# Weighted layer of a four-layer graph network: 21 dense blocks of 125 targets instead of 22, and 61 gathered groups instead of 60

## The reference, cut to what matters

```
msgs = x[src] * edge_weight[:, None]
agg  = segment_sum(msgs, dst, num_segments=6250)
out  = concat([x, agg], axis=-1) @ mlp_w.T + mlp_b
x    = layernorm(x + out)
```

## Time and profile before

| | |
|---|---|
| median of three runs | 3292.46 us |
| profiled execution, time / span | 3296.23 us / 3294.4 us |
| PE busy over the span | 2884.0 us (88%) |
| POOL busy over the span | 2196.1 us (67%) |
| DVE, ACT busy | 1772.5 us (54%), 1134.6 us (34%) |
| weighted stage, first gather to first result product | 1509.40 to 2142.84 us |

### The profile page before, as it was taken

One profiled execution on the slowest core, in us unless ns is written; L12 is line 12 of the kernel. 1 busy time (PEld: TensorE's weight loads), 2 busy tenths in 40 slices (PEclk: granted clock), 3 DMA queues, 4 the chain that ended last, 5 costly groups with the idle time before them and its releaser, 6 DMA issues. The chain is left out here.

```text
span 3294.4 us, 63759 instructions
## 1 busy us (share of the span) xinstructions
PE 2884.0 (88%) x23799; PEld 2539.8 (77%) x23799; DVE 1772.5 (54%) x5488; ACT 1134.6 (34%) x1749; POOL 2196.1 (67%) x2185
## 2 busy tenths in 40 slices
PE   1699999999899999997999999987988788877886
PEld 0377777787688878776999999977977777777776
DVE  6899997233433343437777777545433333333333
ACT  2655555000200010105666666534422222222221
POOL 4466652777477757766777777627777777777773
PEclk9799999999999999998999999968988888888886
DMA  7355555787777876772222222123222222222222
GB/s 165 122 189 176 200 190 196 265 286 273 246 250 251 286 269 231 264 257 67 47 47 48 48 48 47 39 64 80 55 53 46 53 52 46 54 45 54 53 45 55
DMA packets 163982, 433.29 MB, mean 132 GB/s; under 512 B 63603, under 2 KB 105513, under 8 KB 143580
## 3 DMA queue, kind: packets, MB, share of 16 engines
q1 hardware_dynamic: 93998, 304.72, 25.9%
q0 software_dynamic: 69680, 124.50, 17.2%
HBM read 335.49 MB, written 93.53 MB: 130 GB/s over the span
## 5 line engine op out<-in xcount | busy, mean ns | idle before, releaser
L829 POOL DMA_INDIRECT work_all<-parts_dram,idx_all x768 | 824.0, 1073 | 349.0 <-issue 227.6
L1423 PE MATMUL ps<-arena 128*128 128x288 bf16 x7154 | 1024.7, 288 | 1.2 <-DMA arena<-blocks_dram 1.2
L2045 POOL DMA_INDIRECT arena<-table,idx_all x696 | 660.9, 950 | 283.0 <-issue 210.2
L1423 PEld LDWEIGHTS ps<-arena 128*128 128x128 bf16 x7154 | 712.1, 100 | 176.2 <-DVE arena L1026 1.5
L2387 PE MATMUL ps<-M,arena 128*128 128x96 f32 x1664 | 419.6, 352 | 176.0 <-DVE arena L2256 173.1
L1591 POOL DMA_INDIRECT arena<-table,idx_all x400 | 396.8, 992 | 121.9 <-issue 121.0
L2387 PEld LDWEIGHTS ps<-M,arena 128*128 128x128 f32 x1664 | 320.0, 239 | 195.7 <-issue 194.1
L1838 PE MATMUL ps<-work_all,gathot 128*128 128x245 f32 x1100 | 312.4, 379 | 10.1 <-issue 4.4
L1846 PE MATMUL ps<-arena,X 128*96 128x125 f32 x2156 | 317.0, 272 | 3.1 <-ACT arena L1633 3.1
L1254 PE MATMUL ps<-arena,spare 128*128 128x245 bf16 x975 | 291.8, 306 | 29.8 <-ACT arena L882 17.3
L1846 PEld LDWEIGHTS ps<-arena,X 128*96 128x96 f32 x2156 | 278.3, 164 | 26.7 <-ACT arena L1633 4.6
(11 more groups left out here) (415 smaller groups left out, 4420.1 us busy)
## 6 DMA issues: line engine op xcount, KB each, us to landing
arena<-blocks_dram SPq DMA_DIRECT2D x117, 1568.0 KB
blocks_dram<-arena SPq DMA_DIRECT2D x39, 1568.0 KB, 5.8
arena<-table,idx_all POOLq DMA_INDIRECT x1096, 2.5
parts_dram<-arena SPq DMA_DIRECT2D x28, 504.0 KB, 3.2
work_all<-parts_dram,idx_all POOLq DMA_INDIRECT x768
arena<-eaT_dram SPq DMA_DIRECT2D x10, 624.0 KB, 5.3
eaT_dram<-arena SPq DMA_DIRECT2D x48, 104.0 KB, 2.5
arena<-qtable SPq DMA_DIRECT2D x104, 45.0 KB
```

The source lines that it names most:

```text
L829: eng.indirect_dma_start(out=gat_rows[kk % 3][:, u, :], out_offset=None, in_=parts_dram[:, :], in_offset=bass.IndirectOffsetOnAxis(ap=idx_ ...
L1423: last = nc.tensor.matmul(apply_ps[n % 2], blk[m % 3][:, b, :], Hs[:, b, :], start=b == 0, stop=b == NB - 1)
L2045: eng.indirect_dma_start(out=rows[g % NROW][:, u, :], out_offset=None, in_=table[:, :], in_offset=bass.IndirectOffsetOnAxis(ap=idx_all[:, ...
```

## The change

The block count goes down by one, and the first gathered group moves from 44 to 43. `NODEW` becomes 2625, the built tiles 525 instead of 550, the gathered groups 61. Since 525 is odd, the half-width room for the fp16 column list is rounded up; the pieces of `TAB` behind it move by some words. The positions in `STEPS`, `GROUP_AT`, `EDGE_AT` and `NODE_AT` follow from the constants.

```
-    WBLK, WFIRST = 22, 44
+    WBLK, WFIRST = 21, 43
...
-        wkey, wslo, wslo_h, wwin = in_tab(NTW), in_tab(NTW), in_tab(NTW // 2).bitcast(fp16), in_tab(NTW)
+        wkey, wslo, wslo_h, wwin = in_tab(NTW), in_tab(NTW), in_tab(-(-NTW // 2)).bitcast(fp16)[:, 0:NTW], in_tab(NTW)
```

## The result

The changed kernel takes 3302.43 us (median of nine runs, 3296.95 to 3311.06) against 3292.74 us for the kernel before in the same nine rounds: ratio 1.0035, 95% interval 1.0024 to 1.0045, slower by 9.7 us at the medians. A second set of twelve runs gave 3299.24 against 3293.33 us, ratio 1.0020 (1.0007 to 1.0032), slower by 5.9. The forecast was 4.1 us slower with a range of 3288 to 3304: the sign, the bound and the stated range held, the size was too small. The forecast's own range, 3293 to 3301, holds the second median and not the first; the chances gave 0.66 to a time that cannot be told from no change and 0.23 to slower, and slower came.

The account below looks back on a forecast made before the run. POOL, with no free time, was taken to become the bound, PE's gain turning into waits. + 10.3 - 4.2 - 0.2 - 1.8 = + 4.1 us on the median 3292.46 gave 3296.6 us; range 3288 to 3304.

Parts of the forecast that it names:

- What bounds the kernel: Weighted stage: PE and POOL go at one pace, 10.30 us per group; POOL has no free time and becomes the bound.
- The waits: PE at `sums` in the weighted stage: idle for the DMA in front of most groups, some 20 us in all.
- The first rival: TensorE stays the bound of the weighted stage, so the time falls by 20.0 us to 3272.5; chance 0.07.
- PE's own need: PE's own time for the changed weighted stage, from first gather to `result_product`: 613 us.
- The clock: Rival: PE's waits lower its granted clock; under 0.96 PE is the bound again, at 0.94 the time is 3311; chance 0.11.
- One group more on POOL: Eight more indirect DMAs on POOL in the weighted stage: one more period, + 10.3 us.
- The end: Slack of 6.04 us between POOL's last issue and the last `sums` shrinks to 1.85, swallowing 4.2 us.
- the shorter tail: From the last `sums` to `result_product`: 17 applies instead of 18 behind the last group, 0.2 us less.
- POOL's own stalls: POOL's indirect DMA issues in the weighted stage: fewer key pairs on DVE shorten the 21.6 us of stalls by 1.8 us.
- The second rival: POOL's stalls fade as PE's waits pull builds apart: at most 3272.5, with half the stalls gone 3287.6; chance 0.08.
- Both halves of the step: POOL's stalls: 0.8 us saved outside group 2, and 1.0 us in group 2 where the `hots` come two pairs sooner.
- share of a block: POOL's stalls outside group 2 shrink by one block's part of the 22: 17.0 / 22 = 0.8 us.

Follow-up runs that it names:

- seven_gathers: The changed kernel with 7 indirect DMAs per group instead of 8, the eighth tile summed with the seventh's rows; 3277.95 us, ratio 0.9959.
- blocks22_groups59: The kernel before with gathered groups starting at 45, so 22 blocks and 59 groups; 3288.49 and 3288.48 us in two sets, ratios 0.9990 and 0.9988.
- half_keys: The changed kernel with every second key pair left out on VectorE, so the adjacency is not the right one; 3286.82 us, ratio 0.9982.
- block_less: The kernel before with 21 dense blocks instead of 22 and its 60 gathered groups kept, some edges left out; 3292.23 us, ratio 1.0003.
- group_more: The kernel before with its 22 blocks kept and group 43 added, 61 gathered groups; 3307.33 us, ratio 1.0048.
- half_keys_22: The kernel before (22 blocks, 60 groups) with every second key pair left out, so the adjacency is not the right one; 3290.15 us, ratio 0.9993.

## Why the prediction was right or wrong

*What bounds the kernel: right.* One pace of PE and POOL, with POOL the one that has nothing to spare, was read from the pauses "issue" and the two timelines, against PE's 99%. The waits came to the forecast 20 us, but in 25 of the 61 groups and not in front of most. The first rival (TensorE stays the bound, 3272.5) did not come. PE's own need was overestimated: 613 us in the prediction, 607.0 in seven_gathers. The clock, named as a sign of being wrong, did fall, but did not make PE the bound: for 6.8 and 3.4 us, beside waits of 2.6 and 2.3 us at `sums`, half of full speed (1.2 of 2.4 GHz) was granted (windows, as in the earlier trace rows):

```profile
1573.20:1580.00 6.80, 6.53 (x37) 6.33 (x38) 0.86 (x3) 1.93 (x3) 5.12 (x6) 0.50 0.19 38
1877.00:1880.40 3.40, 3.40 (x15) 2.99 (x14) 0.75 (x3) 0.14 (x1) 2.49 (x4) 0.51 0.26 45
```

The mean from 1540 to 2140 is 0.99, above the 0.96 at which the prediction has PE as the bound; POOL waited 0.3 us for `sums` in all, and the last `sums` idled for the DMA.

*One group more on POOL: right.* Without stalls the issues last 634.3 - 25.2 = 609.1 us against 621.1 - 22.0 = 599.1: + 10.0, forecast + 10.3.

*The end: mis-sized a little.* The last group lands 2.87 and 2.88 us behind its issue, not 1.85. The profiles show mostly 1.6 to 1.8 (at most 3.04) for a waiting group that has another behind it, and 2.87 to 3.14 for the last one in all six that wait for it. The 1.72 was also not the only row before with PE waiting, as the prediction has it: `sums` 11 waited 1.19 us and started 2.79 us after its last issue had ended. So 3.2 and 4.1 us are swallowed (from 6.04 and 6.98), forecast 4.2. The 0.2 us of the shorter tail came (6.31 to 6.15).

*POOL's own stalls: this step failed.* I took 1.8 us off. They grew: 25.2 and 23.5 us against 22.0 and 20.7, + 3.0 at the means, which is 4.8 of the 5.1 us by which the stretch missed the forecast. As two profiles of one kernel differ by up to 3.1 us (blocks22_groups59), that nothing was saved is surer than the size of the growth. The second rival, that the stalls fade, did not come either. Both halves of the step were wrong. Outside the first eight groups the stalls are 17.9 and 16.3 us for 525 key pairs, 15.7 and 16.8 for 550: no share of a block comes off. In the first eight they are 7.3 and 7.2 against 6.4 and 3.9: moving the `hots` two steps forward did not shorten a stall by two pairs; two long issues of 3.5 and 3.0 us stand there in place of a varying one or two. The cause of stalls, the key pairs, was named rightly (half_keys), but one block fewer of them did not shorten the stalls. They lie mostly in runs end to end and, it seems, hang on where an issue falls against a run; this was not shown. Why the order of the changed kernel is worse there than that of block_less (2.7 us) with the same pairs was not tried.

The sum by measured terms, at the means of two profiles each: + 10.0 + 3.0 - 3.6 - 0.2 = + 9.2 us for the stretch (642.5 against 633.3, forecast + 4.1), beside 9.7 and 5.9 us in the times.

*What stays open.* The times of group_more and seven_gathers are 10 and 12 us above what their stretches say, those of the others at most 5; in the profiles of these two and of block_less the part behind the stretch takes 1157.3 to 1158.8 us, where the ten others have 1150.2 to 1152.1. Nothing there was edited. It is why single spans of this kernel do not measure a change of 5 us.

## What to carry to other kernels

An engine at 75% busy can be the bound: look at what its idle time is made of. If each instruction of it is followed by the same short pause that nothing releases, it has nothing to spare, and work may not be moved onto it, even from an engine at 99%. Where two engines go at one pace, take work from the one without giving it to the other, and test each half of a trade by itself; the halves need not add up to the whole. A stall that depends on how two engines' instructions fall against each other does not scale with their number; give it the range that the profile shows, not a share.

## What the runs showed of the hardware

- The issue of an indirect DMA of 128 rows takes 0.944 us plus a pause of 0.30, and up to 4.03 us while VectorE runs key one-hots end to end; with half of the key pairs left out never more than 1.11 (half_keys) and 1.26 (half_keys_22).
- The last indirect DMA of a series is used 2.87 to 3.14 us after its issue ended, one with another behind it mostly 1.6 to 1.8 us after (99 of 133 groups that were waited for; at most 3.04).
